# Moving ACT's first relu, its row norm and half of a second norm inside one block of a fused GNN and mixture-of-experts kernel

## The reference

```python
x = x + gnn(layernorm(x), edge_attr_96, u, W1, b1, W2, b2, (src, dst), batch0)
x = x + ffn(layernorm(x), gate_w, gate_b, w1, b1, w2, b2, gamma, beta)

def gnn(x, edge_attr, ...):          # 6250 nodes x 256, 100000 edges x 96, dst is sorted
    out1 = segment_sum(edge_attr, col)
    out2 = where(cnt > 0, segment_max(edge_attr, col), 0)
    out3 = out1 / maximum(cnt, 1.0)
    h = concatenate([x, out1, out2, out3, u[batch]], axis=1)
    return relu(h @ W1 + b1) @ W2 + b2 + x      # hidden width 1024

def ffn(x, ...):                     # 16 experts, top 2 of each row, hidden width 512
    weights, experts = softmax(top_k(x @ gate_w + gate_b, 2))
    moe = sum over the two chosen e of weight_e * (relu(x @ w1[e] + b1[e]) @ w2[e] + b2[e])
    return layernorm(x + moe) * gamma + beta
```

## Time and profile before

| | |
|---|---|
| median of 3 runs | 1272.97 us |
| the profiled execution: its time | 1271.26 us |
| its span, first to last instruction | 1269.4 us |
| PE, ACT, POOL, DVE busy | 86%, 51%, 64%, 66% of the span |
| mean granted TensorE clock | 0.925 |

### The profile page before, as it was taken

One profiled execution on the slowest core, in us unless ns is written; L12 is line 12 of the kernel. 1 busy time (PEld: TensorE's weight loads), 2 busy tenths in 40 slices (PEclk: granted clock), 3 DMA queues, 4 the chain that ended last, 5 costly groups with the idle time before them and its releaser, 6 DMA issues.

```text
span 1269.4 us, 27454 instructions
## 1 busy us (share of the span) xinstructions
PE 1097.0 (86%) x6460; PEld 955.6 (75%) x6461; DVE 832.5 (66%) x3164; ACT 647.6 (51%) x1974; POOL 807.2 (64%) x1056
## 2 busy tenths in 40 slices
PE   2002999999999999999999999889999999999935
PEld 1002888888888888887888788789999999999911
DVE  4989999899989989980367811366322222247788
ACT  5863565566556656665566534222323232345554
POOL 4886657666666666666676525556666566657586
PEclk7555999999999999998999999899999999999975
DMA  9995768777776785479111146776666676688855
GB/s 318 282 306 181 256 232 311 253 271 286 268 259 249 293 259 204 169 286 315 54 38 47 30 154 203 261 250 200 204 209 213 205 217 214 208 295 293 282 178 155
DMA packets 131327, 282.70 MB, mean 223 GB/s; under 512 B 25900, under 2 KB 38576, under 8 KB 131114
## 3 DMA queue, kind: packets, MB, share of 16 engines
q1 hardware_dynamic: 94230, 218.41, 50.2%
q0 software_dynamic: 26048, 43.47, 11.3%
q10 hardware_dynamic: 10964, 19.96, 4.6%
HBM read 167.27 MB, written 114.25 MB: 222 GB/s over the span
## 4 chain that ended last, share of the span: by engine, by line
PE 57%; POOL 11%; issue 10%; DMA 8%; ACT 7%; DVE 3%; POOLq 2%; ACTq 1%; SPq 0%; DVEq 0%
PE ps L1299 16%; PE ps L1307 15%; PE ps L1188 7%; PE ps L1174 7%; PE ps L1176 6%; DMA mem<-piece_carry,mem 4%; DMA mem<-in_dst_dram,mem 2%; POOL mem L639 2%; POOL mem L640 2%; POOL mem L622 2%; PE ps L1285 2%; ACT mem L926 1%; POOL mem L791 1%; PE ps L1178 1%; POOL mem L797 1%
## 5 line engine op out<-in xcount | busy, mean ns | idle before, releaser
L1026 ACT ACTIVATE mem<-ps,mem 128x128 f32<-128x128 f32 x452 | 129.3, 368 | 284.6 <-PE ps L1299 283.8
L1299 PEld LDWEIGHTS ps<-mem 128*128 128x128 f32 x1808 | 220.6, 194 | 18.9 <-issue 12.2
L1299 PE MATMUL ps<-mem 128*128 128x128 f32 x1808 | 224.8, 278 | 10.2 <-issue 9.6
L1174 PE MATMUL ps<-mem 128*128 128x250 f32 x800 | 209.3, 384 | 11.7 <-ACT mem L926 10.0
L1307 PE MATMUL ps<-mem 128*128 x904 | 214.8, 381 | 0.7 <-issue 0.7
L1396 DVE TENSOR_TENSOR_SCAN mem<-ps,mem 128x80 f32<-128x80 f32 x960 | 208.0, 304 | 0.3
L1400 DVE TENSOR_TENSOR_SCAN mem<-ps,mem 128x80 f32<-128x80 f32 x960 | 207.9, 308 | 0.0
L1176 PE MATMUL ps<-mem 128*128 128x250 f32 x800 | 205.0, 379 | 0.0
L1188 PE MATMUL ps<-mem 128*125 128x256 f32 x800 | 182.4, 381 | 0.7 <-ACT mem L926 0.7
L1307 PEld LDWEIGHTS ps<-mem 128*128 128x128 f32 x904 | 163.8, 191 | 18.8 <-issue 0.9
L1174 PEld LDWEIGHTS ps<-mem 128*128 128x128 f32 x800 | 153.3, 194 | 31.6 <-ACT mem L926 12.3
(11 more groups left out here) (284 smaller groups left out, 1677.2 us busy)
## 6 DMA issues: line engine op xcount, KB each, us to landing
mem<-in_L_ffn_w_dram SPq DMA_DIRECT2D x129, 512.0 KB, 9.4
run_sum<-mem SPq DMA_DIRECT2D x80, 480.0 KB
run_max<-mem SPq DMA_DIRECT2D x80, 480.0 KB
mem<-in_edge_attr_dram SPq DMA_DIRECT2D x72, 480.0 KB, 8.2
mem<-expert_rows SPq DMA_DIRECT2D x26, 256.0 KB, 5.5
x_rows<-mem ACTq DMA_DIRECT2D x25, 256.0 KB, 4.4
x_normed<-mem ACTq DMA_DIRECT2D x25, 256.0 KB
mem<-in_x_dram ACTq DMA_DIRECT2D x24, 256.0 KB
```

The source lines that it names most:

```text
L1026: ins = act.activation(hT[b][:, c, :], bank(2 + b, c * P, (c + 1) * P), ACT.Relu, bias=eb1c[:, bass.ds(e, 1), c])
L1174: pe.matmul(h, W1x[:, c, hc * P:(hc + 1) * P], XT[b][:, c, :], start=(c == 0), stop=False)
L1299: ins = pe.matmul(bank(2 + b, f * P, (f + 1) * P), w1now[q][:, c, f * P:(f + 1) * P], XgT[b][:, c, :], start=(c == 0), stop=(c == DC - 1))
```

## The change

Only ACT's order changes, in three places; what is computed is the same, and so is each instruction. First, `carry_in(i+1)` goes from before `relu(i, 0)` to behind it and `take_logits`. Second, the two activations that make the first norm's rows (L912 before) leave `mask_rows` and become `norm_rows`, directly behind `carry_in`; node_rows is now set by the last masked copy. Third, the second part of `moments2(i-1)` goes from directly behind the first to behind `mask_rows`, in front of `relu(i, 1)`.

```diff
+            def norm_rows(i, g, b):
+                act.wait_ge(rstd1_ready, i + 1)
+                for a in range(2):
+                    act.activation(XN[b][:, a, :], XR[b][0:NT, a, :], ACT.Identity, bias=nmr_1[:, a:a + 1], scale=rstd_1[:, a:a + 1])
+
             def mask_rows(i, g, b):
                 act.wait_ge(joined, i + 2)
                 for a in range(2):
                     j = bass.ds(2 * (MACROS - 1 - i) + a, 1)
                     act.activation(NB[b][:, a, 0:2 * EF], RAW[b][:, a, :, :].rearrange("p s f -> p (s f)"), ACT.Identity, scale=has[:, j])
                     act.activation(NB[b][:, a, 2 * EF:2 * P], RAW[b][:, a, 0, 0:EF - REST], ACT.Identity, scale=rch[:, j])
-                    act.activation(NB[b][:, a, 2 * P:3 * P].rearrange("p (n r) -> p n r", n=QUAD), spread(RAW[b][:, a, 0, EF - REST:EF], 1, QUAD),
-                                   ACT.Identity, scale=rch[:, j])
-                act.wait_ge(rstd1_ready, i + 1)
-                for a in range(2):
-                    ins = act.activation(XN[b][:, a, :], XR[b][0:NT, a, :], ACT.Identity, bias=nmr_1[:, a:a + 1], scale=rstd_1[:, a:a + 1])
+                    ins = act.activation(NB[b][:, a, 2 * P:3 * P].rearrange("p (n r) -> p n r", n=QUAD), spread(RAW[b][:, a, 0, EF - REST:EF], 1, QUAD),
+                                         ACT.Identity, scale=rch[:, j])
                 ins.then_inc(node_rows, 1)
...
                     moments1(*after(i, g, b), 0)
                     moments1(*after(i, g, b), 1)
-                    carry_in(*after(i, g, b))
                 relu(i, 0)
                 if logit:
                     take_logits(i - 2)
+                if more:
+                    carry_in(*after(i, g, b))
+                if more:
+                    norm_rows(*after(i, g, b))
                 if norm:
                     moments2(i - 1, 0)
-                    moments2(i - 1, 1)
                 if not isinstance(i, int) or i + 2 < MACROS:
                     act.wait_ge(residual_ready, 2 * i + 2)
                     load_x(i + 2, b)
                 if more:
                     mask_rows(*after(i, g, b))
+                if norm:
+                    moments2(i - 1, 1)
                 relu(i, 1)
...
             carry_in(0, 0, 0)
+            norm_rows(0, 0, 0)
             mask_rows(0, 0, 0)
```

## The result

The changed kernel takes 1316.21 us (median of 4, 1315.07 to 1318.04) against 1272.97: a ratio of 1.0345 (95% interval 1.0319 to 1.037). It is 43 us slower, where 60 were forecast; 1316 lies inside the range. The profiled execution took 1315.52 us, 44.3 more than that of the kernel before.

A forecast was written before the change was run, and what follows sets the result against it. PE and an equally long round through POOL and ACT bound the step; 24.83 - 12.15 + 11.96 + 3.78 = 28.42 us a round over 22 rounds gave 61 us more, 1333 us, range 1304 to 1360.

The forecast's parts named there:

- hardly a wait in it: Claim that the one POOL and ACT round read before the change, 24.83 us, contains almost no waiting.
- the round: One turn through POOL and ACT, norm2's end to norm2's end: 24.83 us before, 28.42 forecast after the change.
- the ring: POOL's norm2, gather, add_rows, then ACT's work up to the sums norm2 needs: bounds the step, 24.83 us.
- mean gather: Time from norm2's end to the gather's last issue on POOL, averaged over all rounds: 11.96 us.
- the three pieces: ACT's norm_rows 1.08, load_x issue 0.85 and masked copies 1.85, now ahead of norm2's sums: 3.78 us a round.
- the join adds no wait: POOL's join ends 2.45 us after the carry, within ACT's 3.0 us of work, so masked copies wait no longer.
- The carry behind the relu: First edit on ACT: costs nothing in the POOL and ACT round, lets PE's relu start earlier; 19 us at most.
- late landings: Rounds whose gather lands late, up to 6.8 us after last issue: up to 0.7 us possible saving, taken as 0.
- PE and ACT alone: Rival: POOL does not bound the step, which is 25.7 us; 1281 us, up to 1300; chance 0.09.
- R + 10.5 + 7.3 + 7.5: PE's step from first relu at R: second relu's first piece, layer2, next first half; next relu put at R + 25.6.
- The clock: Rival: PE's 2.5 us waits bring the low clock for longer, 33.3 us a step; 1388 us; chance 0.05.
- Faster: Rival: PE sets the step and its relu no longer waits for gathers; up to 19 us less, 1254; chance 0.04.

The follow-up runs named there:

- e2: The kernel before with only the third edit, moments2's second part moved behind load_x, masked copies and row norm: 1323.71 us, ratio 1.0415.
- e3: The changed kernel with its third edit undone, both parts of moments2 together ahead of load_x and the masked copies: 1292.33 us, ratio 1.0171.
- e9: The changed kernel with POOL's gather cut from six issues to four from block 2 on: 1272.49 us, ratio 0.9972 to the kernel before.
- e10: The kernel before with POOL's gather cut from six issues to four from block 2 on: 1255.59 us, ratio 0.986.
- e14: The kernel before with moments1 ahead of store_x1 and the head of POOL's gather ahead of norm2: 1250.71 us, ratio 0.982.
- e1: The kernel before with only the first edit, the carry moved behind the first relu and the logits: 1281.85 us, ratio 1.0082.
- e12: The kernel before with the head of POOL's gather (level read, index copy) ahead of norm2: 1256.21 us, ratio 0.9855.

## Why the prediction was right, and where its size was off

The view of what bounds the changed kernel held. The split put work into a ring that had hardly any slack: e2 shows the loss with the split alone, e3 shows it mostly gone without, and e9 shows most of it gone when POOL's part is shortened with ACT's order untouched.

Of the kernel before, "hardly a wait in it" is true of the round that I read and of eight others. In the other 13 POOL waited for take_g, so the ring did not set the step there. Without that wait the ring is 11.9 + 4.4 + 6.0 + 2.1 = 24.4 us (mean gather, to the end of moments1, the usual stretch to the end of the sums, to norm2's end), as long as the 24.41 us that e10 and e14 show for a step of PE (24.7 in the prediction). The mean round was 25.67 us from norm2's end to norm2's end, because in different rounds now a late gather and now PE came last. In the changed kernel it is 27.78: the stretch with the three pieces is 3.15 us longer on average (9.65 for 6.50), the wait for take_g gives 0.85 back (0.03 for 0.88), and the gather and the rest give 0.2. That the forecast needed no term for this slack was in part luck: it took one full round and added the pieces to that.

The mis-sized term is the round: 28.42 us forecast, (765.59 - 154.78) / 22 = 27.76 measured. 22 x 0.66 is 15 us, and that is the distance between +61 and the +46 of the relus of step 23. Of the 0.66, the three pieces make 0.24: they added 9.56 - 6.02 = 3.54, not 3.78. Row by row they are 351.88 to about 352.86 (0.98, not 1.08, since activations overlap at their ends), 0.92 and 1.77, together 3.67; the other instructions of the stretch took 0.13 less. The 0.92 ended with POOL's join and not with the issue of load_x, although I had said that the join adds no wait: over 115 to 820 us the masked copies wait 22.7 us for it, in 25 steps.

The mean gather makes 0.16 more of the 0.66: 11.80 over the 22 rounds of the changed kernel, not 11.96. The rest, 0.26, is one term: from the end of the sums to norm2's end the round that I had read takes 2.26 us, and the mean over the 22 rounds of the changed kernel is 2.01. (Two smaller things cancel: moments1 is shorter in the rounds written out after the loop, 2.8 us and not 3.1, and a few rounds have a late landing.) So the size was off mainly because two parts were read from a single round. The last 2 us lie outside the rounds: the changed kernel reaches the relu of step 1 earlier by 0.8 us, and from that of step 23 to the end it needs 1.3 us less.

The carry behind the relu: "costs nothing in the ring" was right, and as an edit for PE alone it was right that it gives nothing; e1 puts it at +0.8%. That late landings are worth 0 in the ring was too low: e2, in which the carry still stands ahead of the relu, takes 7 us more than the changed kernel, 28.12 us a round against 27.78.

PE's side: a step of 25.6 to 25.8 by PE and ACT alone came out for e1 (25.7), where node_rows is 10 us behind the relu; for the changed kernel's own order e9 shows 25.1 to 25.2. The terms written there, R + 10.5 + 7.3 + 7.5, come to R + 25.3 and not to 25.6. I had the turn waiting 0.3 to 0.5 us a step, and in the row shown it starts within 0.2 us of the last masked copy (over all the rounds PE waits there twice, 1.1 us together); the second relu is 0.4 us late, as forecast (0.5).

The clock: I feared slow stretches behind waits of 2.5 us in every step. PE's waits were shorter, 0.7 to 2.8 us, and slow stretches did come, more than before. Between 155 and 766 us the changed kernel has ten stretches at the lower clock, the kernel before four; each of the ten begins in or close behind a wait for the first relu. Here are one of them, the longest, and the second half shown above, which follows a wait of 2.14 us (the order of the values is that of rows 9):

```profile
596.50:600.00 3.50, 3.35 (x8) 2.79 (x9) 0.00 (x0) 3.35 (x12) 1.70 (x4) 0.51 1.09 353
```

```profile
238.00:245.00 7.00, 5.50 (x13) 4.54 (x14) 5.23 (x14) 6.17 (x21) 4.76 (x9) 0.51 1.03 407
```

```profile
348.50:357.00 8.50, 7.94 (x43) 6.57 (x44) 2.87 (x10) 7.49 (x25) 4.05 (x8) 1.00 0.83 321
```

A stretch of 3.5 us at half the clock costs PE 1.7 us, the ten together 19 us. The rival fell all the same, because they fit into the time that PE has left: the ten rounds with such a stretch take 27.9 us on average, the other twelve 27.7. From 160 to 765.6 us the granted clock was 0.97, where the kernel before had 0.98 over its rounds. The rival "PE and ACT alone" fell too: add_rows never waited for take_g in the 22 rounds. "Faster" needed a round under 24.7 us.

## What to carry to other kernels

Before moving an instruction on one engine, follow the chain from it through the other engines' queues until it comes back, and add up the ring: a ring as long as the step is a bound though no engine in it looks busy. What an engine does before it releases such a ring costs its full length in every turn, what it does right after may cost nothing; and a head of work that needs nothing from the wait in front of it belongs in front of that wait. When one wait is removed, look what is late next: here it was the turn, norm2's rows, the join or the landing, and only where the gathers themselves were issued earlier was hardly anything late (e12), or nothing (e14).

## What the runs showed of the hardware

An indirect DMA costs POOL 1.21 to 1.33 us each plus 0.30 us between two, whatever lands (96 or 192 columns): the issue, not the data, fills 9 of the gather's 12 us. Its landing, counted from the last issue, went from under 4.0 to 7.6 us in rounds of the same kernel (a cut waited 3.56 us in the changed kernel's second round). TensorE's clock did not follow the length of the wait alone: of the changed kernel's twenty waits for the first relu between 155 and 766 us, ten (0.84 to 2.76 us) were followed by a stretch at the lower clock, mostly of 3.5 to 4 us, and ten (0.72 to 2.25 us) were not. In the kernel before one of 2.46 us was followed by 6.5 us at 0.55.
